# One transformer layer on one core: weight forms kept in DRAM between two passes, and down products in seven instead of eight

## The reference, cut to what matters

```python
gate_w = gate_t.astype(jnp.float32) * gate_s[:, None]     # gate_t, up_t: [3584, 1024], values -1, 0, 1
up_w = up_t.astype(jnp.float32) * up_s[:, None]
down_w = down_t.astype(jnp.float32) * down_s[:, None]     # down_t: [1024, 3584]
gate_out = x_flat @ gate_w.T
up_out = x_flat @ up_w.T
hidden = jax.nn.silu(gate_out) * up_out
out_flat = hidden @ down_w.T
x = _layernorm(x + out_flat)
```

## Time and profile before

| what | value |
|---|---|
| median of 3 runs | 1897.69 us (1897.24 to 1906.5) |
| profiled execution: its own time | 1897.28 us |
| profiled execution: span from first to last instruction | 1895.5 us |
| mean granted TensorE clock | 0.991 of full |
| instructions | 27786 |
| moved by DMA | 210.61 MB |

### The profile page before, as it was taken

How to read it: one execution, slowest core, us unless ns; L and a number is a source line. 1 busy time by engine, 2 the same in 40 slices (tenths; PEclk the granted TensorE clock), 3 DMA queues, 4 the chain that set the end, 5 groups by cost and what they waited for, 6 DMA issues and landing times.

```text
span 1895.5 us, 27786 instructions
## 1 busy us (share of the span) xinstructions
PE 1823.7 (96%) x10592; PEld 891.2 (47%) x10592; DVE 1134.5 (60%) x2028; ACT 771.0 (41%) x1166; POOL 504.8 (27%) x999
## 2 busy tenths in 40 slices
PE   7989999999999988889999999999999999999997
PEld 4545655555556533334444444444444444444443
DVE  7877778678767764446445444656545444545555
ACT  5343444445434444345333343342453433334421
POOL 1354556446546555230000000202200000002214
PEclk9999999999999999999999999999999999999999
DMA  8443234324324396455222132449331322214201
GB/s 247 112 105 75 60 87 129 73 68 135 81 54 117 94 218 211 163 175 189 84 80 89 56 112 81 142 136 209 134 126 64 105 74 89 78 56 156 89 12 78
DMA packets 228020, 210.61 MB, mean 111 GB/s; under 512 B 183856, under 2 KB 184112, under 8 KB 227888
## 3 DMA queue, kind: packets, MB, share of 16 engines
q1 hardware_dynamic: 227024, 208.45, 38.1%
q10 hardware_dynamic: 864, 0.39, 0.1%
HBM read 133.03 MB, written 39.85 MB: 91 GB/s over the span
## 4 chain that ended last, share of the span: by engine, by line
PE 86%; DVE 5%; issue 2%; POOL 2%; SPq 2%; ACT 2%; DMA 1%; ACTq 0%; DVEq 0%; POOLq 0%
PE bank L868 34%; PE bank L883 20%; PE bank L774 19%; PE bank L822 4%; PE bank L786 3%; PE bank L810 3%; PE bank L833 2%; PE bank L789 1%; SPq L1354 1%; DVE row_max L1055 1%; POOL p_tiles L1234 1%; DVE xT_parts L1019 1%; DMA x_forms_spill<-x_parts 0%; DVE stats L1010 0%; ACT weight_forms L969 0%
## 5 line engine op out<-in xcount | busy, mean ns | idle before, releaser
L868 PE MATMUL bank<-x_forms,weight_forms 128*128 128x512 f16 x3136 | 702.6, 380 | 18.7 <-DVE up_blocks L1155 6.5
L868 PEld LDWEIGHTS bank<-x_forms,weight_forms 128*128 128x128 f16 x3136 | 306.1, 98 | 392.9 <-issue 14.0
L883 PE MATMUL bank<-w_down,hid 128*128 128x512 f16 x1792 | 408.3, 379 | 3.1 <-DVE hid L1172 3.1
L936 ACT ACTIVATE p_tiles<-bank 128x512 f32<-128x512 f32 (+1 forms) x352 | 193.2, 557 | 288.7 <-PE bank L810 285.0
L883 PEld LDWEIGHTS bank<-w_down,hid 128*128 128x128 f16 x1792 | 175.2, 98 | 215.0 <-DVE hid L1172 4.0
L1055 DVE TENSOR_REDUCE row_max<-bank 128x1 f32<-128x384 f32 (+3 forms) x352 | 219.6, 635 | 94.1 <-PE bank L789 93.1
L1260 POOL TENSOR_TENSOR acc<-acc,down_scale 128x1024 f32<-128x1024 f32 x16 | 38.9, 2431 | 765.3 <-DVE acc L1193 765.3
L774 PE MATMUL bank<-wq_parts,xT_parts 128*128 128x256 f16 x1536 | 217.7, 275 | 9.0 <-DVE wq_parts L1019 8.7
L1226 POOL TENSOR_SCALAR_AFFINE_SELECT p_tiles<-p_tiles 128x128 f32<-128x128 f32 (+2 forms) x352 | 137.8, 400 | 215.0 <-ACT p_tiles L936 214.3
L774 PE MATMUL bank<-wo_parts,att_parts 128*128 128x512 f16 x768 | 191.2, 381 | 2.0 <-DVE row L1104 1.4
L774 PEld LDWEIGHTS bank<-wq_parts,xT_parts 128*128 128x128 f16 x1536 | 144.3, 98 | 56.3 <-issue 13.9
(11 more groups left out here) (105 smaller groups left out, 1771.9 us busy)
## 6 DMA issues: line engine op xcount, KB each, us to landing
w_page<-gateT SPq DMA_DIRECT2D x56, 512.0 KB, 4.4
w_page<-upT SPq DMA_DIRECT2D x56, 512.0 KB, 4.6
w_page<-downT SPq DMA_DIRECT2D x56, 512.0 KB, 4.7
x_forms_spill<-x_parts SPq DMA_DIRECT2D x56, 256.0 KB, 2.5
att_spill<-att_made SPq DMA_DIRECT2D x64, 128.0 KB, 2.1
att_parts<-att_spill SPq DMA_DIRECT2D x16, 512.0 KB, 3.4
x_row<-x_spill SPq DMA_DIRECT2D x16, 512.0 KB, 3.5
out<-acc SPq DMA_DIRECT2D x16, 512.0 KB, 2.7
```

The costliest lines, as they stand in the source:

```text
L868: t = nc.tensor.matmul(strassen[bank_set(use)][to][:, :], w_form[:, use % 4, A_FORMS[a_form], k * P:(k + 1) * P], xF[:, :, B_FORMS[b_form] ...
L883: t = nc.tensor.matmul(to[:, :], hid[g % 2][:, c, a, i % 2, i // 2 * P:(i // 2 + 1) * P], w_down[:, g % 2 * GC + c, cols], start=g == grou ...
L936: nc.scalar.activation(p32[j][:, h0:h0 + heads, :], bank[5 + m % 2][:, 0:heads * n].rearrange("p (h c) -> p h c", c=n), ACT.Exp, scale=SCO ...
```

## The change: what it does

1. **Weight forms in DRAM.** In the first pass, when a use's seven forms are there, they are stored (`w_store`, 128 x 3584 f16). In the second pass they are loaded (`w_in`) in place of being made: no int32 page, no cast, no `w_form` there. The down weights of a round are stored (`d_store`) and loaded (`d_in`, 128 x 2048 f16) likewise.
2. **Down products by seven.** In the first ten rounds of the second pass the down products of a round are Strassen's too: [two row blocks x two chunks] times [two chunks x two column halves]. It needs seven forms of the hidden block (three more hi and three more lo; four differences and sums on POOL, `hid_form`) and seven of the weights (four operations on DVE, `d_form`). A part takes two rounds: 4 pairs of tiles x 7 products x 4 matmuls. Each product's bank is added to one block of `acc`. The last four rounds, and the first pass, keep plain down products.
3. **Waits at the end of attention.** The first weight pages and casts wait for `scores_over`, which leaves out exponentials, masks, sums and value products; the first products no longer wait for the last scaling of attention (only use 5 does); the copies still wait for `attention_over`. The last value product goes to bank 3 and waits for the last row maximum instead of for the scaling before it.
4. **Memory.** Hidden forms and down weights lie in a ring of three places (in the first pass and the last rounds: four places in the same memory). `down_scale`, `x1_row` and `last_down` lie in it as well, so that `down_scale` is loaded once per pass, behind the down products of an earlier part. `gate_blocks` and `up_blocks` changed places. A constant in the scale of the hidden block (`HID_BOUND`) is four times as large, which leaves room for the sums of blocks.

The diff, cut to its core:

```diff
+ND = 6
+PLAIN = 2 * (ND - 1)
+DOWN_ROUNDS = [list(range(p * NF + 2 * d, p * NF + (2 * d + 2 if d < ND - 1 else NF))) for p in range(PASSES) for d in range(ND)]
+DOWN_OF = {r: q for q, rounds in enumerate(DOWN_ROUNDS) for r in rounds}
...
+DOWN_PRODUCTS = [(False, "A11", "B11", (0, 0)), (False, "S1", "T1", (1, 1)), (True, "S2", "T2", (0, 1)), (True, "S4", "B22", (0, 1)),
+                 (True, "S3", "T3", (1, 1)), (False, "A12", "B21", (0, 0)), (True, "A22", "T4", (1, 0))]
+DOWN_B = {"B11": 0, "T3": 1, "B21": 2, "B22": 3, "T1": 4, "T2": 5, "T4": 6}
+DOWN_MADE = ["T1", "T3", "T2", "T4"]
+HID_FORMS = ["A11", "S3", "A22", "S1", "S2", "A12", "S4"]
+HID_MADE = ["S3", "S1", "S2", "S4"]
...
+def plain(n):
+    return n < NF or n % NF >= PLAIN
...
+def room_after(n):
+    p, r = divmod(n, NF)
+    if p == 0:
+        return DOWN_OF[r - 4] if r > 3 else None
+    return DOWN_OF[p * NF + min(r - 3, PLAIN - 1)] if r > 2 else p * ND - 1
...
+            for _ in range(4 if n < NF else 10):
+                if left and DOWN_ROUNDS[left[0][0]][-1] < n:
                     down_at[left.pop(0)] = clock
-                    clock += one
-        while n % NF == NF - 1 and left and DOWN_GROUPS[left[0][0]][-1] <= n // 2:
+                    clock += one if n < NF else one / 2
...
+            if form in HID_MADE:
+                made = {"S3": [("hidden", n, 1)], "S1": [("hidden", n, 2), ("hid_form", n, "S3")], "S2": [("hid_form", n, "S1")],
+                        "S4": [("hid_form", n, "S2"), ("hidden", n, 3), ("hid_lo", n, "S3")]}[form]
+                put(PO, at[form] - 1.4, 1.35, "hid_form", n, form, after=made)
+            put(SC, at[form], .65, "hid_hi", n, form, after=[("hidden", n, k) if k is not None else ("hid_form", n, form)] + room + (
+                [("hid_hi", n, forms[f - 1])] if f else []))
+            put(VE, at[form] + .7, .75, "hid_lo", n, form, after=[("hid_hi", n, form)] + before)
...
+    for n in range(NF):
         for w in range(2):
-            pages += [(w, n + 1, c) for c in range(2) if n + 1 < ROUNDS] + [(2, n // 2, n % 2 * 2 + w)]
+            pages += [(w, n + 1, c) for c in range(2) if n + 1 < NF] + [(2, n, w)]
...
+            put(SY, at + 6, .4, "w_store", use, moves=FORMS_MOVE, after=[("w_form", use, 3)])
...
+    for n in range(NF, ROUNDS):
+        for use in range(2 * n, 2 * n + 2):
+            put(SY, use_at[use] - 20, .4, "w_in", use, moves=FORMS_MOVE, after=[ended(use - 4, NPR - 1), ("w_store", use - 2 * NF)] + (
+                [("w_store", use - 4)] if use - 4 < 2 * NF else []))
+        at, old = use_at[2 * n + 1] - 6, room_after(n)
+        put(SY, at, .4, "d_in", n, moves=PAGE_MOVES, after=[("d_store", n - NF), ("down", *DOWN_LAST[old])] + (
+            [("acc", *DOWN_LAST[old])] if old == ND - 1 else []))
+        if not plain(n):
+            for k, form in enumerate(DOWN_MADE):
+                put(VE, at + 6 + .5 * k, .45, "d_form", n, form, after=[("d_in", n)] + ([("d_form", n, DOWN_MADE[k - 1])] if k else []))
...
+        def place_free(on, n):
+            old = room_after(n)
+            if old is not None:
+                on.wait_ge(s_down, DOWN_N[DOWN_LAST[old]] + 1)
+            on.wait_ge(s_last, 2 * PT * (n // NF))
...
+        def scores_over(on):
+            on.wait_ge(s_proj, PROJ_LAST_Q)
+            on.wait_ge(s_sk, NU * NKEY)
+            stacked(on, len(rot_n) - 1)
+            for n in range(MROWS):
+                on.wait_ge(s_mrow[n], 16 * NU)
...
+                    if j == NT - 1 and q == NU * UG - 1:
+                        on.wait_ge(s_max, NU * NROW)
+                    elif j == NT - 1:
...
+                    if n >= NF:
+                        on.wait_ge(s_win[use % 4], 16 * ((use - 2 * NF) // 4 + 1))
+                    elif i < 2:
                         on.wait_ge(s_cast, cast_n["w_cast", w, n, 0])
-                    on.wait_ge(s_wform, 4 * use + (0, 0, 1, 2, 3, 4, 4)[i])
+                    else:
+                        on.wait_ge(s_wform, 4 * use + (0, 0, 1, 2, 3, 4, 4)[i])
...
-                    on.wait_ge(s_scale_att, 4 * NU * UG)
...
+                        pair, i = divmod(m, NPR)
+                        added, a_form, b_form, _ = DOWN_PRODUCTS[i]
+                        for r in rounds:
+                            on.wait_ge(s_hlo, lo_n(r, a_form))
+                            if b_form in DOWN_MADE:
+                                on.wait_ge(s_dform, dform_n["d_form", r, b_form])
+                            else:
+                                on.wait_ge(s_din[(r - NF) % 4], 16 * din_n(r))
+                            for a in range(2):
+                                t = nc.tensor.matmul(to[:, :], hid_f[r % NF % 3][:, HID_FORMS.index(a_form), a, pair * P:(pair + 1) * P],
+                                                     wd_f[r % NF % 3][:, DOWN_B[b_form], :], start=not added and r == rounds[0] and a == 0,
+                                                     stop=r == rounds[-1] and a == 1, skip_group_check=True)
...
+                            on.wait_ge(s_wst[use % 4], 16 * (use // 4))
...
+                    elif n:
+                        if w == 0:
+                            on.wait_ge(s_hform, hform_n["hid_form", n - 1, "S2"])
+                            on.wait_ge(s_hlo, lo_n(n - 1, "A22"))
+                        else:
+                            on.wait_ge(s_hlo, HID_BASE[n])
...
+                elif kind == "d_form":
+                    n, form = which
+                    b = wd_f[n % NF % 3]
+                    on.wait_ge(s_din[(n - NF) % 4], 16 * din_n(n))
+                    on.wait_ge(s_dform, dform_n["d_form", n, form] - 1)
+                    to, left, right, op = {"T1": (4, 1, 0, ALU.subtract), "T3": (1, 3, 1, ALU.subtract),
+                                           "T2": (5, 1, 0, ALU.add), "T4": (6, 2, 5, ALU.subtract)}[form]
+                    nc.vector.tensor_tensor(b[:, to, :], b[:, left, :], b[:, right, :], op).then_inc(s_dform, 1)
...
+                elif kind == "hid_form":
+                    n, form = which
+                    _, to = hid_of(n, form)
+                    k = hform_n["hid_form", n, form]
+                    on.wait_ge(s_hid, 4 * n + {"S3": 2, "S1": 3, "S2": 3, "S4": 4}[form])
+                    if form == "S3":
+                        nc.gpsimd.tensor_tensor(to, gate_t[:, 0, :], gate_t[:, 1, :], ALU.subtract).then_inc(s_hform, 1)
+                    elif form == "S1":
+                        nc.gpsimd.tensor_tensor(to, gate_t[:, 1, :], gate_t[:, 2, :], ALU.add).then_inc(s_hform, 1)
+                    elif form == "S2":
+                        on.wait_ge(s_hform, k - 1)
+                        nc.gpsimd.tensor_tensor(to, up_t[:, 1, :], gate_t[:, 0, :], ALU.subtract).then_inc(s_hform, 1)
+                    else:
+                        on.wait_ge(s_hform, k - 1)
+                        on.wait_ge(s_hlo, lo_n(n, "S3"))
+                        nc.gpsimd.tensor_tensor(to, gate_t[:, 3, :], up_t[:, 2, :], ALU.subtract).then_inc(s_hform, 1)
...
+                elif kind == "w_in":
+                    use = which[0]
+                    on.wait_ge(s_prod, PRODUCT_N[use - 4, NPR - 1])
+                    for i in range(4):
+                        on.wait_ge(s_wst[i], 16 * len(range(i, min(2 * NF, use - 2 * NF + 1), 4)))
+                    on.wait_ge(s_wst[use % 4], 16 * len(range(use % 4, 2 * NF, 4)))
+                    e.dma_start(w_form[:, use % 4, :, :].rearrange("p f c -> p (f c)"), wF_dram[use - 2 * NF]).then_inc(s_win[use % 4], 16)
+                elif kind == "d_in":
+                    n = which[0]
+                    place_free(on, n)
+                    for i in range(4):
+                        on.wait_ge(s_dst[i], 16 * len(range(i, NF, 4)))
+                    to = wd_p[place_of(n)].rearrange("p c d -> p (c d)") if plain(n) else wd_f[n % NF % 3][:, 0:4, :].rearrange("p f c -> p (f c)")
+                    e.dma_start(to, wd_dram[n - NF]).then_inc(s_din[(n - NF) % 4], 16)
```

301 lines of the change are left out of this document (191 added, 110 removed).

## The result

The changed kernel takes 1889.98 us (median of 8 runs, 1886.17 to 1895.27) where the kernel before takes 1897.52 (8 runs): ratio 0.9954, 95% interval 0.9935 to 0.9973. It is faster by 7.5 us, 0.4%; forecast were 1874.5 us and a gain of 23, and the range ended at 1889. All runs that are compared here were in the faster state. The profiled execution took 1892.16 us, its span 1890.4; that of before 1897.28 and 1895.5.

A forecast was written before the change was run, and what follows sets the result against it. TensorE's matmuls were taken to bound the kernel, 1823.7 us busy of a 1895.5 us span. The sum: 1897.3 - 17.3 - 3.5 - 5 + 3 = 1874.5 us, range 1862 to 1889.

The forecast's parts named there:

- (a): Down products of ten second-pass rounds: seven products for eight remove 80 matmuls at 0.216 us each, -17.3 us.
- (d): Cost of the seven products in second-pass rounds: 1 us for banks, 2 us for a gate copy's wait, +3 us.
- (b): Boundary of the passes: forms loaded instead of made remove casts ahead of copies, -3.5 us, bounds 0 and -4.0.
- the copy behind its own product: Boundary of the passes: named as next late, the 1.5 us that remain of 5.5 us idle.
- (c): End of attention: new waits let the first page and FFN products start earlier, -5 us, bounds -12 and +2.
- delay a load by half a landing of 4.4 us: End of attention: the bound of +2 us, if the four stores in this stretch hold up a load.
- The load: Seven-product rounds: DVE busy 66% of the time, ACT 28%, POOL 14%; none becomes the bound by load.
- the banks: Two down banks in seven-product rounds: back-to-back pieces lose 0.18 us a pair, 12.6 us if all 70; 1 us taken.
- rival B: Seven-product rounds: POOL's hidden forms and DVE's lo parts lock each other out, 6 to 12.5 us; 1878.5 to 1885, chance 0.22.
- C: SP's queue: waiting loads stand still until forms come 3 us late in each part, +15 us, 1889.5; chance 0.08.
- D: Seven-product rounds: down pieces wait for DVE's adds, 0.93 us per pair, 65 us in all, 1936; chance 0.05.
- A: Transitions give more: -12 us at the end of attention, -4.0 at the boundary, no stalls, 1864; chance 0.12.

The follow-up runs named there:

- E1: Not a run: the event in a profile where TensorE starts the 256 down matmuls that end pass one; it divides the span.
- E2: Not a run: the event in a profile where TensorE starts the 256 down matmuls that end pass two; it divides the span.
- plain_downs: The changed kernel with plain down products in all rounds, weight forms still stored and loaded: 1896.43 us.
- again: The changed kernel once more, unedited: 1889.36 us.
- few_stores: The changed kernel without storing the weight forms of the first 24 uses; the second pass reads the last four uses' forms instead: 1880.33 us.
- late_stores2: The changed kernel with the stores of the first six uses planned later, no sooner than the fourth product of the use after next; all bytes stored: 1879.77 us.
- S: Not a run: the event in a profile of the last score product of attention on TensorE; it divides the span.
- small_stores2: The changed kernel with the same order and waits, but stores of the first 24 uses carrying one form of seven: 1888.38 us.
- no_pool_forms2: The changed kernel without the 40 POOL operations that make hidden forms; products read what the tile holds: 1881.69 us.
- late_plain: The changed kernel with the stores of the first six uses planned later and plain down products in all rounds: 1886.6 us.

## Why the prediction was wrong, point by point

- **(a), seven products for eight, -17.3 us:** the count is right, 1712 matmuls for 1792. From E1 to E2 the interval less its idle time is 528.7 us in plain_downs and 513.6 in "again", 15.1 less. The other 2.2 us are waits too. By the distances between the starts of matmuls, 0.216 us each at a clock of 1.00, "again" loses 12.3 us in ten gaps and plain_downs 3.6 in two. Idle figures leave out some 0.16 us of each gap, as the records overlap, 1.3 us for eight gaps more, and five gaps of under 0.5 us in "again" add 0.7. All this belongs to (d).
- **(b), the boundary, -3.5 us within 0 and -4.0:** measured -3.5 in plain_downs and -3.8 in "again": size and cause were right. The three waits behind the casts are gone. What is late next is a load of x_forms, 0.85 us in "again", 1.18 in plain_downs and 1.32 in the change's first profile, besides the 0.79 that was there before; the forecast had named the copy behind its own product.
- **(c), the end of attention, -5 us within -12 and +2:** as a sum this failed, by 6 to 7 us. The early start gave its 3.5 to 4.7 us, but the stores that share the stretch cost 7.5 (few_stores) to 9.3 (late_stores2) there, so that the part came to some +1.2 (S to E2 is 10.0 us shorter in "again" than before: -17.3 - 3.5 + 9.6 + 1.2; with the boundary counted by gaps as in (a), -4.3, it is +2.0). The step that failed is the bound "delay a load by half a landing of 4.4 us", and that nothing of it went into the -5: I priced a store by its transfer, and small_stores2 shows that the transfer is worth 1.0 us or nothing. What costs is where all other work goes when a planner with fixed queues gives each store 3.3 us of the DMA queue, and the clock that falls after the waits. That the part still lies within +2 is luck: two terms that cancel, of which the bound had one, and mis-sized. The forecast's first product before 746 us came true, the idle time of about 20 us did not (27.3, and 25.9 in "again").
- **(d), what the seven products cost, +3 us:** measured 17.3 - 7.7 = 9.6. The load was right (DVE 66%), and so were the banks: acc adds stand in none of PE's waits there, though 1 us of the +3 was put down for them. The step that failed is the reading of the earlier trace rows in rival B, "0.27 us, not POOL's whole 1.27", and with it that durations of DVE stay as the trace of before has them. There the two engines seldom met, so a median of 0.687 said nothing of what happens when they do; where they meet, an operation of 0.68 us took 1.75. The trace of before shows it already, in one of the sixteen instructions of the earlier trace rows:

```profile
734.43 1.26 POOL L1279 TENSOR_TENSOR row<-row,x_difference 128x512 f32<-128x512 f32 x1
...
735.30 0.94 DVE L1122 SCALAR_TENSOR_TENSOR x_parts<-x_difference,x_parts 128x512 f16<-128x512 f32 x1 [3.02 <-ACT x_parts L948]
```

  POOL ends at 735.69 and DVE 0.55 us later, at 736.24, the same 0.54 to 0.56 as in the turns above. It came late into POOL's 1.26 us, and so it lost 0.25 us and not more: the excess is what is left of POOL's instruction, not a price of its own. Others of L1122 in that trace, on other tiles than the one that I asked for, took up to 1.31 (at 673.30), also ending 0.55 us behind POOL. Of the 9.6 us, 7.2 go with POOL's forms (E1 to E2 524.2 to 517.0) and 4.8 can be had back with everything computed (519.4). The 2.4 us that stay without POOL's forms are, but for 0.4, two waits of PE for a sum, in no_pool_forms2 0.66 us at 1362.40 and 1.34 at 1762.76, which plain_downs does not have; what causes them stays open.
- **The rivals.** B was right in its mechanism. Its 6 us stand beside the 7.2 of E1 to E2 by luck, since its place was another: S2 on POOL, done at 1378.41, was not what came late, but DVE's own lo parts, stretched, ahead of the gate's sum in DVE's queue. The Trainium skill (SBUF — State Buffer, the section "SBUF: two separate sides") says that a DVE operation with two SBUF inputs and a POOL operation that reads SBUF lock each other out for a whole instruction; the turns at 1375 to 1379 us agree, and its rule, not my median, was the one to price with. C and D did not come: among PE's waits from 1345 us in "again" there is none for a weight form's DMA or for an acc add. A's -12 at the end of attention is not reached even with late stores, where (c) comes to 1.2 - 9.3 = -8.1.
- **By the sum:** of -22.8 forecast, (c) is 6.2 us short and (d) 6.6, which leaves -10.0 where the medians differ by 7.5 to 8. Of the rest 1.6 us lie in the last column of the table, 66.4 or 68.0 us. Both values occur among kernels that hold the change, and in runs with the same order on every engine ("again" 68.0, small_stores2 66.4); of the kernel before there is one trace, with 66.4. Two kernels with plain down products show it in the timeline of PE:

```profile
1826.61 55.41 PE L1043 MATMUL bank<-down_forms 128*128 128x512 f16 x256 [2.43 <-issue]
```

```profile
1820.55 57.10 PE L1043 MATMUL bank<-down_forms 128*128 128x512 f16 x256 [2.44 <-issue]
```

The same 256 matmuls after the same idle time take 55.4 us in plain_downs and 57.1 in late_plain; the granted clock of the first 7.5 us was 1.00 there and 0.77 here, between the two levels. Single profiles thus carry 1.6 us that medians average.

## What to carry to other kernels

When a change adds work to POOL beside DVE operations that read two SBUF tiles, price every such overlap as one engine waiting for the other, however seldom the trace of before shows it; four forms of 0.68 us on the busy engine were cheaper here than the same four on an idle one. When work goes into a plan with reckoned queue times, price the order that comes out, not the bytes (here 3.3 us reckoned for 0.3 cost 6.4 at equal bytes): it is worth one experiment with the new transfers planned late. And take a term apart by parts that can go wrong separately; two opposite terms of 5 and 8 us in one sum came out as nearly nothing.

## What was not expected of the hardware

- A DVE operation and a POOL operation that both read SBUF took turns: 1.75 us for 0.68 on DVE, 1.59 and 1.64 for 1.27 on POOL, over a stretch of many such pairs 886 ns for 682 on average. The delayed DVE operation ended 0.54 to 0.56 us after POOL's, in the trace of before as in that of the change.
- A store of 896 KB from SBUF takes 7.4 us to land, the load of the same bytes 4.6; and 71 GB/s more, mostly of stores (93 to 164), cost PE nothing in the steady first pass (358.00 us busy of 358).
- After 2.4 us of idle time the granted clock fell in some executions (0.77 over the 7.5 us behind it) and stayed at 1.00 in others, with the same work before it: 57.1 or 55.4 us for the same 256 matmuls.
